# Two-layer transformer on one core: the values' products of the local transformer split into even and odd heads, and the exponents of a gate step moved into the next step

## What is computed

```python
for i in range(6):
    x = attn_layer(shift_tokens(x), Wqkv[i], q_scale[i], k_scale[i], Wo[i]) + x
    x = ffn_layer(shift_tokens(x), ln_g[i], ln_b[i], W1[i], b1[i], W2[i], b2[i]) + x

# attn_layer: 16 heads of 64, windows of 32 tokens
q, k, v = split(x @ Wqkv)
q, k = rotary(l2norm(q) * qs), rotary(l2norm(k) * ksc)
# each window of queries sees the window before and its own: 64 keys
sim = einsum('bhwie,bhwje->bhwij', bq, bk2) * 8
attn = softmax(where(mask, -max, sim), -1)
out = einsum('bhwij,bhwje->bhwie', attn, bv2)        # "values weighed"
return out @ Wo

# ffn_layer
xn = (x - mu) / sqrt(var + 1e-05) * g + bln
a, gate = split(xn @ W1 + b1)
return a * gelu(gate) @ W2 + b2
```

## Time and profile before

| | us |
|---|---|
| median of 3 runs | 2621.43 (2620.44 to 2627.61) |
| the profiled execution | 2632.24 |
| its span, first to last instruction | 2630.4 |

### The profile page before, as it was taken

The page is one execution under the profiler, slowest core; times in us unless marked ns, Lnnn a source line. Parts: engine busy times, 40 slices in busy tenths (PEclk is TensorE's granted clock), DMA queues, the critical chain, the costliest instruction groups (busy, mean ns, idle before and its releaser), DMA issues. The chain is left out here.

```text
span 2630.4 us, 118521 instructions
## 1 busy us (share of the span) xinstructions
PE 2464.2 (94%) x52349; PEld 1960.7 (75%) x52349; DVE 2173.0 (83%) x2455; ACT 2024.8 (77%) x4031; POOL 1538.0 (58%) x1075
## 2 busy tenths in 40 slices
PE   6799999999999999999999999689999999997999
PEld 2478888888887888888788888467776776775787
DVE  5788888888888888888898887388988898985888
ACT  4688888888888888888888887566766676764676
POOL 3788888888888878888897776022322232322111
PEclk8899999999999999999999999899999999999999
DMA  3243433443443334434433333121322222221221
GB/s 99 53 94 92 105 77 92 93 107 81 95 96 99 79 94 97 103 84 94 96 95 78 83 81 75 32 60 43 68 58 61 48 64 56 61 50 37 82 72 41
DMA packets 275792, 202.00 MB, mean 77 GB/s; under 512 B 117568, under 2 KB 215880, under 8 KB 274248
## 3 DMA queue, kind: packets, MB, share of 16 engines
q1 hardware_dynamic: 275280, 194.42, 30.9%
HBM read 36.96 MB, written 1.11 MB: 14 GB/s over the span
## 5 line engine op out<-in xcount | busy, mean ns | idle before, releaser
L509 POOL TENSOR_TENSOR lt_t_sin<-lt_qk,lt_tab 128x512 f32<-128x512 f32 x384 | 682.7, 1799 | 235.5 <-DVE lt_qk L1278 233.0
L514 POOL TENSOR_TENSOR lt_qr<-lt_qr,lt_t_sin 128x1024 f32<-128x1024 f32 x192 | 458.5, 2388 | 28.7 <-POOL lt_t_sin L509 1.3
L2058 DVE TENSOR_REDUCE fa_neg_max<-bank 128x1 f32<-128x1024 f32 x256 | 301.6, 1220 | 93.4 <-PE bank L1855 91.7
L1980 ACT ACTIVATE fa_prob<-bank,fa_neg_max 128x1024 f32<-128x1024 f32 x128 | 142.7, 1115 | 219.1 <-DVE fa_neg_max L2058 166.9
L1881 PE MATMUL bank<-fa_prob_t,fa_v 32*64 32x128 f32 x16384 | 292.8, 276 | 15.6 <-issue 10.9
L2068 DVE STREAM_TRANSPOSE fa_prob_t<-fa_prob 128x1024 f32<-128x1024 f32 x256 | 302.1, 1218 | 0.0
L1881 PEld LDWEIGHTS bank<-fa_prob_t,fa_v 32*64 32x64 f32 x16384 | 243.9, 130 | 76.4 <-issue 55.9
L602 PE MATMUL bank<-lt_w_high,lt_x_high 128*128 128x512 f32 x576 | 279.9, 486 | 1.3 <-POOL lt_x_low L486 0.5
L1278 DVE TENSOR_TENSOR lt_qk<-lt_qk,lt_rn 128x2048 f32<-128x2048 f32 x96 | 252.0, 2625 | 22.6 <-ACT lt_rn L991 21.3
L619 PE MATMUL bank<-ident,lt_qr 128*128 128x128 f32 x1536 | 234.2, 276 | 13.8 <-POOL lt_qr L514 9.8
L970 ACT COPY lt_qk<-bank 128x512 f32<-128x512 f32 x384 | 229.5, 599 | 17.4 <-POOL lt_t_sin L509 3.8
(11 more groups left out here) (259 smaller groups left out, 5927.0 us busy)
## 6 DMA issues: line engine op xcount, KB each, us to landing
lt_v<-lt_v_tok SPq DMA_DIRECT2D x576, 128.0 KB
fa_v<-fa_v_tok SPq DMA_DIRECT2D x256, 128.0 KB, 2.7
lt_v<-lt_v_tok SPq DMA_DIRECT2D x192, 64.0 KB
lt_k_t<-lt_k_t SPq DMA_DIRECT2D x84, 128.0 KB, 2.7
lt_v<-lt_v SPq DMA_DIRECT2D x168, 64.0 KB, 2.1
lt_w_raw<-in_lt_wqkv_dram SPq DMA_DIRECT2D x36, 256.0 KB, 3.5
ex_cw_all<-cw_kept SPq DMA_DIRECT2D x8, 1024.0 KB, 4.6
lt_x_s<-h_in SPq DMA_DIRECT2D x96, 64.0 KB, 2.7
```

Of the source, the lines that this page charges most:

```text
L509: pool.tensor_tensor(dst[:, :, i, :], src[:, :, 1 - i, :], tab[:, g // 2 % 2, 1, at:at + 32].unsqueeze(1).to_broadcast([P, HEADS, 32]), AL ...
L514: pool.tensor_tensor(qr[:, g % 2, half], qr[:, g % 2, half], t_sin[:, :], ALU.add).then_inc(S.rotated, 1)
L2058: dve.tensor_reduce(neg_max[:, u % 2, par:par + 1], bank[:, 2 * par:2 * par + 2, :].rearrange("p a n -> p (a n)"), AX.X, ALU.max, negate=T ...
```

## The change

Four edits:

- `weigh_v(g)` becomes `weigh_v(g, par)` and is called twice in step i. The first call, for the even heads, stands where the only one stood and has its waits. The second, for the odd heads, is the last thing of the step, behind centering or up products and behind the output products. Each signals S.av.
- `load_v` on SP waits for both calls of the block before (the count is doubled), and `norm_att(g, par)` on DVE waits for the call of its own parity.
- The exponents of a gate step are not taken at its end on ACT, but in the next step, after the attended values are emptied and a weight cast, if there is one, and before `square_qk`.
- In that next step DVE sums the probabilities after the first `shift_scores` instead of before it.

```diff
--- before.py
+++ after.py
@@ -375,7 +375,7 @@
                         sp.wait_ge(S.cleared, 5)
                         sp.wait_ge(T.sum, NCH)
                     if g >= 2:
-                        sp.wait_ge(S.av, g - 1)
+                        sp.wait_ge(S.av, 2 * (g - 1))
                     if has_look(g):
                         for par in range(2):
                             lo = HD * par
@@ -660,23 +660,24 @@
                                           prob[:, g % 2, 4 * n + i, :, :].rearrange("p a k -> p (a k)"), ident[:, :])
                     mm.then_inc(S.prob_turned, 1)
 
-                def weigh_v(g):
-                    pe.wait_ge(S.prob_out, 2 * (g + 1))
-                    pe.wait_ge(s_v[g % 2], 8 * 16 * (g // 2 + 1))
-                    if has_look(g):
-                        pe.wait_ge(S.look, looks(g))
-
-                    if g >= 1:
-                        pe.wait_ge(S.av_out, 2 * g)
-                    if live(g + 1):
-                        pe.wait_ge(S.shifted, 2 * (g + 1) + 1)
+                def weigh_v(g, par):
+
+                    if par == 0:
+                        pe.wait_ge(S.prob_out, 2 * (g + 1))
+                        pe.wait_ge(s_v[g % 2], 8 * 16 * (g // 2 + 1))
+                        if has_look(g):
+                            pe.wait_ge(S.look, looks(g))
+
+                        if g >= 1:
+                            pe.wait_ge(S.av_out, 2 * g)
+                        if live(g + 1):
+                            pe.wait_ge(S.shifted, 2 * (g + 1) + 1)
+                    f = slice(64 * par, 64 * par + 64)
                     for hp in range(PAIRS):
                         for w in range(WPB):
-                            for par in range(2):
-                                f = slice(64 * par, 64 * par + 64)
-                                mm = pe.matmul(bank[WIN * w:WIN * w + WIN, value_bank(g, par), hp * HD:(hp + 1) * HD],
-                                               prob_t[f, g % 2, hp, WIN * w:WIN * w + WIN],
-                                               v[f, g % 2, w, hp, :], start=True, stop=True)
+                            mm = pe.matmul(bank[WIN * w:WIN * w + WIN, value_bank(g, par), hp * HD:(hp + 1) * HD],
+                                           prob_t[f, g % 2, hp, WIN * w:WIN * w + WIN],
+                                           v[f, g % 2, w, hp, :], start=True, stop=True)
                     mm.then_inc(S.av, 1)
 
                 def turn_att(g, n):
@@ -941,7 +942,7 @@
                     if live(i + 1):
                         project_v(i + 1, 1)
                     if live(i - 1):
-                        weigh_v(i - 1)
+                        weigh_v(i - 1, 0)
                     if even(i, 4) is not None and i != ALL + 2:
                         center(even(i, 4))
                     if even(i, 5) is not None:
@@ -954,6 +955,8 @@
                         last_var(2)
                     if live(i - 2) and i - 2 < ALL - 1:
                         project_out(i - 2)
+                    if live(i - 1):
+                        weigh_v(i - 1, 1)
 
             @blk.scalar
             def _(act):
@@ -1201,6 +1204,8 @@
                     for k in splits_at(i):
                         if k % WCH < 4:
                             split_high(k)
+                    if live(i - 1) and even(i - 1, 5) is not None:
+                        exponent(i - 1)
                     if live(i + 2):
                         square_qk(i + 2, 0)
                     if live(i - 1):
@@ -1224,7 +1229,7 @@
                         second_log(2)
                     if live(i + 1):
                         empty_v(i + 1, 1)
-                    if live(i):
+                    if live(i) and even(i, 5) is None:
                         exponent(i)
                     if i == ALL + 1:
                         last_square(0)
@@ -1314,7 +1319,7 @@
                 def norm_att(g, par):
                     if par == 0:
                         dve.wait_ge(S.inv_sum, g + 1)
-                    dve.wait_ge(S.av, g + 1)
+                    dve.wait_ge(S.av, 2 * g + par + 1)
                     r = row_sum[:, g % 2, :].rearrange("p (h a) -> p h a", a=2)[:, :, par:par + 1]
                     dve.tensor_tensor(att[:, g % 2, :, par, :],
                                       bank[:, value_bank(g, par), :].rearrange("p (h d) -> p h d", d=HD),
@@ -1530,10 +1535,12 @@
                     if i == 0:
                         second_scale(3)
                         modulation(1)
-                    if live(i - 1):
+                    if live(i - 1) and even(i - 1, 5) is None:
                         sum_probs(i - 1)
                     if live(i):
                         shift_scores(i, 0)
+                    if live(i - 1) and even(i - 1, 5) is not None:
+                        sum_probs(i - 1)
                     if i == ALL + 1:
                         last_sum(0)
                         last_sum(1)
```

## The result

| | before | after |
|---|---|---|
| median, us (runs on one chip, side by side) | 2624.52 (4 runs, 2620.44 to 2631.06) | 2661.85 (4 runs, 2656.38 to 2674.53) |
| ratio of the times | | 1.0134, 95% interval 1.0113 to 1.0155 |
| the profiled execution, us | 2632.24 | 2656.38 |
| its span, us | 2630.4 | 2654.5 |

The changed kernel is slower, by 37 us between the medians. The forecast was 2664 us, slower, with a range from 2612 to 2712. In the changed kernel `weigh_v` stands at L678, the up products at L722 and L723, centering at L708, the output products at L700 and the exponents at L1032; scores and turned probabilities keep L648 and L659.

What follows compares the result with a forecast made beforehand. PE was taken to set the pace in the local transformer's steps. Terms 71 - 30 - 8 - 4 + 14 gave +43 us, hence 2664 us from the 2621.4 median, with a range of 2612 to 2712.

Steps and rivals of the forecast that it cites:

- Two halves on four tiles: Values' products on PE: two halves of 1.03 us plus second entry replace 1.41 us, +71 us (bounds +55 to +157).
- Breaks at the values' group: Instruction breaks in the values' products on PE mostly vanish, -30 us (0 to -36); lost clock behind them, -8 (0 to -15).
- Waits for POOL: PE's load-side waits for POOL's rotated queries and keys, 7.2 us, shrink as PE comes later: -4 us (0 to -7).
- Late exponents: PE waits for ACT's exponents before turning probabilities in even steps, longer where a weight cast stands ahead: +14 us (0 to +27).
- Sums on DVE: Sums of probabilities and a reciprocal move into DVE's idle time before L1349, costing nothing.
- SP, 0: Later loads of values, f_x and next x on SP's queue cost nothing; 0 to +5 us, taken as 0.
- a new wait on f_x: Sign against the reasoning: it is wrong if PE has new waits on av, f_x or values.
- stay: Breaks at the scores, 11.0 us of PE idle time before L648, remain because nothing around L648 moves.
- (a): Fetch decides and turns faster, breaks at L648 go too: -26 us, 2595, or about 2610 with part of it; chance 0.14.
- (b): It cancels out within 8 us: tiles +60, all L677 breaks gone, no wait for exponents; chance 0.12.
- (c): Four tiles of one row half do not overlap their loads: rounds of 0.084 us, +129 us, 2750; chance 0.07.
- (d): First half's group also breaks into supply pauses: +0.1 us a half, 2684 us, inside the forecast; no chance given.

Runs made afterwards that it cites:

- the kernel with head pairs: Kernel before with values' products split at the same two places by head pairs, both parities in each half; 2617.55 us against 2629.12, ratio 0.9959.
- the split alone: Kernel before with only the values' products split into even and odd heads, exponents left as before; 2650.70 us against 2629.12, ratio 1.0091.
- two tiles: Kernel before with windows as outer loop of the values' products, so neighbours use only two tiles; 2740.27 us (one run) against 2627.79.
- the group with parity outside: Kernel before with parity as outer loop of the values' products, one group at the old place; 2644.37 us against 2627.79, ratio 1.0062.

## Why the prediction was right

The sum was +43 us; between the medians it is +37, in the section +29. By its own terms, with 93 groups counted and carried to 96 steps:

1. *Two halves on four tiles, +71.* Measured: the halves' median is 1.028 us, where 1.03 was worked out, and the second entry 0.093 us, where 0.09 was. Together 2.15 for 1.41, +0.74 a step, **+71**. This term is right to the microsecond, and the kernel with head pairs shows its cause: same places, eight tiles, 33 us less than the split alone. It is not the full 71 (that kernel's halves also enter the mode twice, and their sum, 2 x 0.79, is over 1.41): its halves are together 44 us shorter, and some 9 of these come back as waits before the transposes and at the scores.

2. *Breaks at the values' group, -30 and -8 for the clock.* The mean of a group over its undisturbed length was 0.40 us, and is 0.01 us in the halves: -0.38 a step, **-37**, with the clock loss inside the groups already in it. The granted clock from 150 to 1640 us went from 0.994 to 1.000; 0.6% of 1490 us is 8.5 us, the 8 of the forecast. Six halves of 182 still ran 0.09 to 0.44 us long there, 1.2 us in all, so the tenth that I gave back was hardly needed. Behind the groups, up products became 11 ns shorter on average (L721 408 ns, now L722 397).

3. *Waits for POOL, -4.* The wait is gone in full, 7.2 us on PE's load side and 1.4 on PE: right in kind, too small. From the last projection product to the transposes of queries and keys the section has 9 us less.

4. *Late exponents, +14.* The order of events was right, the wait stands at L659 and is longest where a cast stands ahead (0.61 us idle, 0.68 lost). PE's idle time there is 8.7 us in 18 steps, with 15.2 us at its loads in 31. From the last score to the first turned probability the section has 12.0 us more. The size is right, the make-up less so: I had 9 us in every even step and 13 more at the casts, less what lies beside breaks. Measured, 9.9 us stand in 18 even steps with a cast and 1.4 in all the others, where the exponents come nearly in time. I also only half had how cheap the move is by itself: 4.5 us, since it then covers the waits for POOL and part of the breaks, and its full price only with the split, which removes both.

5. *Sums on DVE, 0,* and 6. *SP, 0.* The sums left no wait on PE. For f_x there is the one wait at 1651 us, 1.9 us and nearly as much again in clock: within the 0 to +5 of the forecast, though a new wait on f_x was also named as a sign that the reasoning is wrong. One step in 95 doesn't overturn it.

What I got wrong is small. The idle time at the scores did not "stay": 11.0 us became 6.3, and 6.7 in the split alone, although nothing around L648 moved. In time it did stay: from first to last score the section takes 136.3 us before, 137.0 after and 137.2 in the split alone. What the breaks gave back, slower records took: the median group of scores with what follows it takes 1.41 us before, 1.51 in the split alone, and 1.52 to 1.54 in the four other kernels that end the step with a dense group, against 1.42 in the two that only slow the group at its old place. The supply of instructions would explain it; no run here shows the cause. The average step was forecast at 16.7 us and is 16.43, from 16.12: the forecast was the plain sum on a step that I took too long, and the step grew by 0.31 us instead of 0.45.

Where the 29 us of the section stand can be measured in full, by summing on PE from start to start by line: values' products +28.7 (two halves for one group, less the breaks), output products +8.1 (the second entry), scores up to the turned probabilities +12.8, up products -7.3 (the clock and short breaks behind the old groups), projections -13.9 (before transposes of queries and keys 9 of it, the waits for POOL), the rest +0.9. The forecast for the first two and the up products was 71 - 30 - 8, +33, and they come to +30; for the exponents +14 and +13. The term that was mis-sized is the relief in the projections, -4 forecast and -14 found. Apart from some 4 us that makes up the difference between +43 and the section. The +37 between the medians is nearer to the forecast, and part of that is luck of the draw: the one trace of before is of an execution slower than its median, and what it had too much may stand in the same places as the relief.

Of the rivals, (a), the fetch decides, had the right size for the breaks at the values (they fell by 37) but nothing to win at the scores, whose time stayed, and failed because the tiles cost their 71 and not the 55 of the bound. The kernel with head pairs comes nearest to it: it has the fetch's relief without the price of the tiles, and gains. (b), no change, fell with it. (c), loads that do not overlap within a row half, asked for 1.4 us or more in a half and 2750 us in all; 1.03 us and the round of 0.056 with four and with two tiles exclude it. (d), pauses in the halves, hardly occurred: mean and median of a half agree within 0.01 us.

## What to carry to other kernels

Before reordering small tiled products, count over how many tiles of the array a run of neighbours is spread: here no tile took more than a record per 0.056 us, and four or two tiles took no less, so the same 128 records took 1.41 us on eight tiles, 2.06 as two halves of four and 3.13 on two. Breaks for instructions became fewer by what stands before and between dense groups, and need not be paid for with such an order; but look for the waits that the new place uncovers. And cost two edits together where one adds a wait and the other removes idle time: a late result is cheap as long as it hides under a wait that the other edit is about to remove.

## What the runs showed of the hardware

- *A dense group pays for the fetch by its place.* The same undivided group of 64 products (128 matmul records and 128 loads) had 24.8 us of idle time on issue behind the values' projection, 3.7 us behind up and output products and 0.9 us with the output products moved ahead. A break's place is set by the record count from the start of the program: all 312 breaks of eleven traces stand on one grid of 125.97 matmul records, within 2.2. Whether one occurs there differs from kernel to kernel, and the condition stays open.
- *Tiles are independent down to two.* Four or two tiles: one record per tile for 0.056 us. Eight tiles keep that pace only for 32 records in 0.25 us; by 0.60 us there are 62, by 0.90 us 93, so 0.010 us a record from then on, which I take for the supply of instructions. At the change from one row half or window to the next, new tiles start before the old ones finish; with leaving the mode only once that saved 0.24 us of 2.06 in the group with parity outside.
- *Entering the tiled mode costs 0.09 us* each time (1.88 us from the output products to the second half, 1.79 to full-width products).
- *What was not tried:* both a split by head pairs and the output products first in one kernel, and anything on the breaks at the scores, which still take 6 to 14 us of idle time in every version.
